# Identity matmuls on TensorE at the changes of stage of an eight-stage kernel, and fewer spreads in an opening

## The reference

```python
x = x + _L0_attn_a_ref(_layernorm(x), Wk, Wq, Wv, Wu, bu)      # softmax attention, 16 heads
x = x + _L0_ffn_ref(_layernorm(x), w12, w3, gate_w)            # 8 experts, 2 chosen
x = x + _L0_attn_b_ref(_layernorm(x), ...)                     # selective scan, 16 states
x = x + _L0_ffn_ref(_layernorm(x), w12, w3, gate_w)
x = x + _L1_attn_a_ref(_layernorm(x), Wq, Wk, Wv, Wo, bo)      # linear attention
x = x + _L1_ffn_ref(_layernorm(x), ...)                        # 16 experts, 4 chosen, and a shared one
x = x + _L1_attn_b_ref(_layernorm(x), ...)                     # gated linear attention
x = x + _L1_ffn_ref(_layernorm(x), ...)
```

## Time and profile before

| | |
|---|---|
| median of 3 runs | 1617.62 us (1616.97 to 1617.71) |
| profiled execution | 1618.38 us |
| its span, first to last instruction | 1616.7 us, 27621 instructions |
| TensorE busy (matmul / load) | 1481.6 us (92%) / 767.3 us (47%) |
| VectorE busy | 1356.7 us (84%) |
| ScalarE busy | 935.5 us (58%) |
| GpSimd busy | 296.0 us (18%) |
| mean granted TensorE clock | 0.953 |
| DMA | 66.13 MB, 41 GB/s over the span |

### The profile page before, as it was taken

How to read it: one execution, slowest core, us unless ns; L and a number is a source line. 1 busy time by engine, 2 the same in 40 slices (tenths; PEclk the granted TensorE clock), 3 DMA queues, 4 the chain that set the end, 5 groups by cost and what they waited for, 6 DMA issues and landing times. The chain is left out here.

```text
span 1616.7 us, 27621 instructions
## 1 busy us (share of the span) xinstructions
PE 1481.6 (92%) x10285; PEld 767.3 (47%) x10285; DVE 1356.7 (84%) x2454; ACT 935.5 (58%) x1763; POOL 296.0 (18%) x352
## 2 busy tenths in 40 slices
PE   7999999999999999799997888877999969989699
PEld 2122222222222221488863333323888758869587
DVE  7999999999999998376656999997776658777686
ACT  3199999999999999532236666653332332222232
POOL 4200000000000000000015878873000200020000
PEclk8599999999999999899998999999999979999799
DMA  3341100000000111000002222210000011300123
GB/s 112 131 127 34 34 27 25 25 25 25 25 25 25 31 38 40 1 1 1 1 1 70 66 68 72 67 66 13 2 1 1 1 47 60 107 1 1 54 86 100
DMA packets 41328, 66.13 MB, mean 41 GB/s; under 512 B 11444, under 2 KB 18661, under 8 KB 40490
## 3 DMA queue, kind: packets, MB, share of 16 engines
q1 hardware_dynamic: 41194, 64.37, 12.9%
HBM read 56.68 MB, written 6.75 MB: 39 GB/s over the span
## 5 line engine op out<-in xcount | busy, mean ns | idle before, releaser
L908 DVE TENSOR_REDUCE row_max<-ps 128x1 f32<-128x1024 f32 x512 | 583.3, 1212 | 13.3 <-PE ps L693 13.3
L814 ACT ACTIVATE probs<-ps 128x512 f32<-128x512 f32 x944 | 505.8, 596 | 55.1 <-PE ps L708 37.8
L693 PE MATMUL ps<-k_stack,q_stack 48*128 48x512 bf16 x1024 | 323.1, 402 | 10.9 <-DVE row_max L908 6.6
L634 PE MATMUL ps<-probs,v_head 128*16 128x256 f32 (+1 forms) x3800 | 314.3, 403 | 5.8 <-issue 5.8
L708 PE MATMUL ps<-q_stack,k_stack 51*128 51x512 bf16 x944 | 287.0, 384 | 0.7
L1440 PE MATMUL ps<-s_hc,ident 128*128 128x512 f32 x256 | 139.8, 632 | 48.5 <-DVE s_hc L1713 43.5
L693 PEld LDWEIGHTS ps<-k_stack,q_stack 48*128 48x128 bf16 x1024 | 60.2, 95 | 256.6 <-DVE row_max L908 240.4
L1087 ACT ACTIVATE x_gate<-ps 128x512 f32<-128x512 f32 x128 | 76.5, 599 | 182.1 <-PE ps L125 182.0
L1365 POOL TENSOR_TENSOR s_dbx<-s_dx,s_b_rows 128x512 f32<-128x512 f32 x128 | 159.6, 1273 | 36.4 <-DVE s_h L1704 35.9
L1704 DVE TENSOR_TENSOR_SCAN s_h<-ps,s_state,s_dbx 128x512 f32<-128x512 f32 x128 | 156.7, 1264 | 4.6 <-POOL s_dbx L1365 2.8
L634 PEld LDWEIGHTS ps<-probs,v_head 128*16 128x16 f32 x3800 | 62.6, 94 | 202.0 <-issue 100.4
(11 more groups left out here) (351 smaller groups left out, 1941.9 us busy)
## 6 DMA issues: line engine op xcount, KB each, us to landing
s_b_rows<-s_b_dram SPq DMA_DIRECT2D x64, 256.0 KB, 3.1
y_spread<-y_probs_dram SPq DMA_DIRECT2D x128, 128.0 KB, 3.0
q_stack<-q_parts_dram SPq DMA_DIRECT2D x30, 96.0 KB
k_stack<-k_parts_dram SPq DMA_DIRECT2D x30, 96.0 KB
w_w<-w_dram SPq DMA_DIRECT2D x1, 2048.0 KB, 7.6
q_stack<-q_parts_dram SPq DMA_DIRECT2D x30, 64.0 KB
k_stack<-k_parts_dram SPq DMA_DIRECT2D x30, 64.0 KB
o_dram<-o_sb SPq DMA_DIRECT2D x60, 32.0 KB
```

The lines of the kernel that those rows point to most:

```text
L634: last = nc.tensor.matmul(core.ps[32 * c:32 * c + VROWS, O_BANK, cut], v_head[buf][:, kt, :], probs[:, m % RING, c * CH:(c + 1) * CH][:, cut],
L693: last = nc.tensor.matmul(core.ps[:, 2 * b + r, :], qst[buf][0:KROWS, u * P:(u + 1) * P], kst[buf][0:KROWS, key:key + CH], start=True, sto ...
L814: nc.scalar.activation(probs[:, us % RING, c * CH:(c + 1) * CH], core.ps[:, S_BANK + n % S_RING, :], ACT.Exp).then_inc(exp_done, 1)
L908: nc.vector.tensor_reduce(mx[:, head % 2, u, b:b + 1], core.ps[:, 2 * b:2 * b + 2, :], mybir.AxisListType.XY, ALU.max).then_inc(max_done, 1)
```

## The change

A helper `keep_busy` multiplies the identity by itself a given number of times into one bank. It is called at six changes of stage (a to x1 with 8 matmuls after a wait for the next norm's variance, x1 to s and x2 to l with 10, s to x2 with 8, y1 to g with 10, g to y2 with 16) and inside the four-chosen opening (4 after a wait for the tanh, 9 after the turn of the weights and, only in linear attention's block, 9 at the end). That makes 62 matmuls at the changes of stage and 35 in the two openings. The second part: SP spreads two pairs (`OPEN_PAIRS`) instead of six in the opening within linear attention; pairs 2 to 5 are issued at the start of the next block.

```diff
--- before.py
+++ after.py
@@ -37,6 +37,7 @@
 
 E1, I1, GROUPS, TOPG, TOP1 = 16, 64, 4, 2, 4
 SCALING = 2.5
+OPEN_PAIRS = 2
 LEVELS = 7
 LEFT = 4
 
@@ -75,6 +76,10 @@
 
     def sb(self, name, shape, dt=F32):
         return self.ctx.enter_context(self.nc.sbuf_tensor(name, shape, dt))
+
+    def keep_busy(self, bank, count):
+        for _ in range(count):
+            self.nc.tensor.matmul(self.ps[:, bank, 0:P], self.ident[:], self.ident[:], start=True, stop=True)
 
     def clear_sems(self, kept):
 
@@ -751,6 +756,8 @@
                                             o_sb[32 * c:32 * c + VROWS, k * P:(k + 1) * P],
                                             w["Wu_last"][32 * c:32 * c + VROWS, :], start=True, stop=True)
                 last.then_inc(last_done, 1)
+            pe.wait_ge(following.var_ready, 1)
+            core.keep_busy(0, 8)
 
         @block.scalar
         def _(act):
@@ -1075,6 +1082,7 @@
                     following.turn(pe, e - 4)
                 down(n - 1)
             down(LAST - 1)
+            core.keep_busy(UP, 10)
 
         @block.scalar
         def _(act):
@@ -1511,6 +1519,7 @@
                 for d in range(ND):
                     add_up(c, DS - 1, d)
             project_out(NC_ - 1)
+            core.keep_busy(C_BANK, 8)
 
         @block.scalar
         def _(act):
@@ -1800,7 +1809,7 @@
 
         @block.sync
         def _(sp):
-            next_stage.open_sync(sp)
+            next_stage.open_sync(sp, OPEN_PAIRS)
 
         @block.tensor
         def _(pe):
@@ -2215,9 +2224,9 @@
         sp.dma_start(pd[c], probsT[:]).then_inc(probs_stored, 16)
         sp.wait_ge(probs_stored, 16 * (c + 1))
 
-    def open_sync(sp):
+    def open_sync(sp, first):
         store_probs(sp, 0)
-        for m in range(P_RING):
+        for m in range(first):
             place_spread(sp, m)
 
     def open_gpsimd(pool):
@@ -2231,9 +2240,14 @@
             if freed is not None and g == SETS - 1:
                 pe.wait_ge(freed, count)
             up(pe, g)
+        pe.wait_ge(tanh_done, 1)
+        core.keep_busy(DOWN, 4)
         turn_probs(pe, 0)
+        core.keep_busy(DOWN, 9)
         pe.wait_ge(probs_copied, 1)
         ln.turn(pe, 1)
+        if freed is not None:
+            core.keep_busy(DOWN, 9)
 
     def open_scalar(act):
         ln.copy_turned(act, 0)
@@ -2264,7 +2278,10 @@
         @block.sync
         def _(sp):
             if with_opening:
-                open_sync(sp)
+                open_sync(sp, P_RING)
+            else:
+                for m in range(OPEN_PAIRS, P_RING):
+                    place_spread(sp, m)
             for c in range(NC_):
                 if c:
                     store_probs(sp, c)
@@ -2312,6 +2329,8 @@
                 down(pe, g)
                 if g + SETS < LAST:
                     up(pe, g + SETS)
+            if following:
+                core.keep_busy(0, 10)
 
         @block.scalar
         def _(act):
@@ -2623,6 +2642,7 @@
             project_out(2)
             turn_o(3)
             project_out(3)
+            core.keep_busy(0, 16)
 
         @block.scalar
         def _(act):
```

## The result

The changed kernel takes **1605.76 us** (median of four runs, 1602.83 to 1607.90), the kernel before, run beside it, 1617.30; the ratio is 0.9929, 95% interval 0.9917 to 0.9942. That is 11.5 us or 0.7% faster, against a forecast of 1607.8 us and a range of 1603 to 1613. The profiled execution took 1606.0 us around a span of 1604.3.

A forecast was written before the change was run, and what follows sets the result against it. Stage borders, where VectorE or once SP's queue is late and TensorE's clock falls, were taken as the limit; 4.0 - 4.1 + 2.9 + 7.0 = 9.8 us gained, forecast 1607.8 us, range 1603 to 1613.

The forecast's parts named there:

- SP's issues: Border from linear attention into y1: with two pairs spread instead of six, the stage starts 4.0 us sooner.
- The clock at y1's start: First units of y1, up to the scores of chunk 1: a held full clock gains 2.9 us, taken whole.
- Inside y2: Low-clock stretch within y2, before the scores of chunk 1: a held clock gains up to 2.5 us.
- 0.65: Share taken of the 10.8 us that a held clock could give outside y1's start: 7.0 us.
- Fills that hold the border: Ends of x1, x2 and y1, and attention to x1: fills delay the border by 1.1, 1.1, 1.6 and 0.3 us.
- The clock at the changes of stage: Five stage changes from x1 to scan through y2's start: a held clock gives up to 1.5, 3.1, 1.4, 1.0, 1.3 us.
- scan to x2: Change from scan to second experts: a held clock gives up to 3.1 us, and the eight fills cost nothing.
- Attention to x1: Change from attention to first experts: a held clock gives nothing, since it had fallen before the fills begin.
- held everywhere: Rival: clock held at all places, 0.1 us lost and 13.7 gained, 1604.0 us; chance 0.22.
- not held: Rival: clock held nowhere, three borders eat the gain of SP's issues, 1617.7 us, the same; chance 0.07.
- slower: Rival: fills at the low clock hold the path in gated attention and both openings, 1627.3 us; chance 0.03.

The follow-up runs named there:

- the parts: Four kernels with parts of the change: pairs only 1611.97 us, fills only 1611.70, pairs and openings' fills 1605.06, fills at changes of stage only 1613.74; before 1617.02.

## Why the prediction was right

The forecast of 9.8 us was within 2 us of the 11.5, and its largest terms were found where it put them. Two of its terms are off in opposite ways, and it is luck that they nearly cancel: y2's inside gave more than was taken, and the fills at the changes of stage gave nothing in the total.

- **SP's issues, 4.0 us**: right. 4.2 us in the trace, 5.0 with the pairs alone, and VectorE waits for no spread in the first units of y1.
- **The clock at y1's start, 2.9 us**: right to the tenth in the trace. That it needs the pairs' part as well was only half said (the prediction let "the two fills of nine leave hardly a pause up to the stage"); the trace of the run with the fills alone shows it.
- **Inside y2, 2.5 us, of which 0.65 was taken**: under-sized. Counted between the meetings of the engines, y2 lasted 109.6 us before and 106.1 to 106.9 in every profile with full-width fills for as long in the openings, but for one of the two of the changed kernel (109.3). With 3.4 us in y1 and 2.8 in y2 that is 6.2 of the 6.9 us that the openings' fills measured, where the forecast had 2.9 + 0.65 x 2.5 = 4.5.
- **Fills that hold the border, 4.1 us**: over-sized, 0.8 + 0.8 + 1.3 and 0.2 at attention to x1: 3.1. The step took the border to follow VectorE's end and TensorE's end alike; GpSimd started 1.64 us behind VectorE and 1.39 behind TensorE. The lengths of x2 bear the 0.8 out: with the same low stretch it takes 160.1 to 160.2 us with the ten and 159.3 without.
- **The clock at the changes of stage, 0.65 of 1.5 + 3.1 + 1.4 + 1.0 + 1.3 us**: the sizes are about right, one factor for all places is not what the traces show. At the three borders with a fill the clock was held in the six traces with full fills there, but for one border (into the scan, with twenty matmuls, where it fell 2.6 us into the stage). The rows show what was foreseen or more (the constant matmuls 1.6 us shorter, the first products of gated attention 1.5). At *scan to x2* it changes from trace to trace: of the seven of kernels with the eight matmuls at this change and none behind x2's turn, the low stretch lasts 6.8 us in one (the one shown above), 3.4 in four and nothing in two; of the three without them it is 6.8 in two and 3.4 in one. Without a fill at its end x2 then takes 160.7 to 160.9 us, 159.3 and 157.7, so the whole 3.1 us were there to be had. How much of it is due to those eight is not settled by these few traces. At y2's start the weights of chunk 0 come about 1.4 us sooner, but in these traces y2 is no shorter with the sixteen (106.9) than with the openings' fills alone (106.4).
- **Attention to x1, nothing**: right in time, 1603.91 us without these eight against 1603.88 with them. In the clock they do show: without them the low stretch is 13.7 to 17.1 us, with them 13.7 in two traces and 10.2 or less in five.
- **The reason given for 0.65** was incomplete. The prediction says that the clock in the middle of stages stays at 1.0 through waits of 0.6 to 1.6 us, and does not name two low stretches in the middle of the scan, 864.8 to 875.0 and 1076.4 to 1083.2 us, which stand behind waits of 2.5 and 2.3 us. The change does not touch them, and they are as long after it.

On top of the openings the fills at the changes of stage were to bring 5.4 - 4.1 = 1.3 us. They brought nothing, and the three at the borders cost about 2 more than they gave. Alone they gained 3.3 us (0.9981), with runs over 8 us. Why they gain alone and not on top of the rest is open: each profile has its other low stretches at other times and of other lengths (the one late in the scan begins between 1068 and 1080 us and lasts 3.4 or 6.8 us), and no run here separates a fill's effect from that shift. One place is seen where a gain is eaten so: in three of the six traces with full fills at all borders (one of them with doubled transposes) the clock falls late in gated attention, and that stage takes 77.2 to 77.5 us, as before; in the other three it does not, and the stage takes 76.1.

The rivals: *held everywhere* (1604.0) is as near to the 1605.8 as the forecast, but scan to x2 was held whole in two traces of seven only; *not held* and *slower* didn't happen with these fills, and the eight-column kernel shows that both mechanisms are real. The Trainium skill (TensorE: Matmul & The Clock Gate, Part 1) says that the clock gate runs free of the kernel's start, so that one kernel differs from run to run; these runs agree, with 2.8 us between the 18 runs of before beside the parts, up to 7.8 us between those of a kernel with fills, and the low stretch of 6.8 or 3.4 us at x2's start in two traces of the same kernel.

## What to carry to other kernels

A fill pays where nothing waits behind it, and where real work follows before the clock can fall: first shorten the wait, then fill what is left. At a border that waits for every engine, a fill that outlasts the slowest engine is on the path, and here it cost as much as the clock gave back or more. Read the stage behind a low stretch before pricing it: from 600 us on the low stretches sum to 93 us before and 44 after, and beside the 5 us of SP's queue only some 6 came off the time. And read more than one trace before calling a place held.

## What was not expected of the hardware

- A float32 matmul with 8 moving columns takes about as long as one with 128 when each has its own 128x128 weights (18 records 2.07 against 2.17 us, of which the loads fill 2.09), but such fills did not keep the clock at 1.0 where those with 128 columns did.
- Float32 transposes keep it as products do, if they fill the same time: 1604.5 us against 1605.8 and 1607.1.
- At a border with two meetings GpSimd starts the stage 1.57 to 1.67 us behind VectorE's last end, or 1.32 to 1.42 behind TensorE's if that is last. At a border with one it is 0.29 and 0.26.
- Two executions of the changed kernel had low stretches of 6.8 and 3.4 us at x2's start, and two other kernels with the same fill there had none.
